# Third attention: scores contract 64 rows in two row halves of the array, 32 keys wide, and the steps go in twos

## The reference, cut to what matters

```python
def _L3_xattn_ref(x, context, Wq, Wk, Wv):      # DIM = 256, NHEADS = 32, HEAD_DIM = 8
    q = x @ Wq.T
    k_raw = context @ Wk.T
    v_raw = context @ Wv.T
    ...
    q = _rmsnorm(q)
    k = _rmsnorm(k)
    scores = jnp.einsum('bhnd,bhmd->bhnm', q, k) * HEAD_DIM ** (-0.5)
    attn = jax.nn.softmax(scores, axis=-1)
    out = jnp.einsum('bhnm,bhmd->bhnd', attn, v)
```

## Time and profile before

| | us |
|---|---|
| median of 3 runs (2715.6 to 2722.59) | 2721.63 |
| the profiled execution | 2722.91 |
| its span, first to last instruction | 2720.8 |
| the 16 pairs of the attention in it, first exponential to end of the last | 526.9 |

### The profile page before, as it was taken

How to read it: one execution, slowest core, us unless ns; L and a number is a source line. 1 busy time by engine, 2 the same in 40 slices (tenths; PEclk the granted TensorE clock), 3 DMA queues, 4 the chain that set the end, 5 groups by cost and what they waited for, 6 DMA issues and landing times. The chain is left out here.

```text
span 2720.8 us, 48003 instructions
## 1 busy us (share of the span) xinstructions
PE 2525.6 (93%) x16164; PEld 1750.9 (64%) x16226; DVE 1721.4 (63%) x3340; ACT 1483.9 (55%) x3294; POOL 1355.3 (50%) x917
## 2 busy tenths in 40 slices
PE   6889999979999999999999999998697799999997
PEld 4567777747777777777777777776454344444443
DVE  4345667657787887787787788786115555554435
ACT  2235444435555566555656655554113667676895
POOL 0025645425666676666667666665102466656300
PEclk9889999999999999999999999998798899999999
DMA  4212222220001000010001000003101000000100
GB/s 155 78 54 85 89 89 76 75 110 16 1 17 45 17 16 17 1 45 17 17 16 44 17 1 17 17 32 154 42 12 58 17 15 17 15 17 15 48 2 16
DMA packets 42437, 108.33 MB, mean 40 GB/s; under 512 B 5044, under 2 KB 26040, under 8 KB 37048
## 3 DMA queue, kind: packets, MB, share of 16 engines
q1 hardware_dynamic: 40424, 102.41, 11.2%
q0 software_dynamic: 768, 2.10, 0.2%
q10 hardware_dynamic: 1008, 0.79, 0.1%
HBM read 99.91 MB, written 4.98 MB: 39 GB/s over the span
## 5 line engine op out<-in xcount | busy, mean ns | idle before, releaser
L1212 POOL TENSOR_TENSOR xn<-xn,l_p 128x512 f32<-128x512 f32 (+1 forms) x400 | 633.9, 1585 | 178.8 <-ACT l_p L1254 162.3
L2213 ACT ACTIVATE l_p<-psum 128x1024 f32<-128x1024 f32 x416 | 394.5, 1022 | 132.6 <-PE psum L2333 132.4
L1340 DVE TENSOR_TENSOR l_plo<-l_p,l_phi 128x512 fp32r<-128x512 f32 (+1 forms) x464 | 405.5, 875 | 63.1 <-ACT l_p L1254 42.4
L1253 ACT ACTIVATE l_phi<-psum 128x512 fp32r<-128x512 f32 (+1 forms) x464 | 279.4, 602 | 221.5 <-PE psum L447 142.1
L1389 DVE TENSOR_REDUCE l_mx<-psum 128x1 f32<-128x512 f32 (+2 forms) x512 | 306.0, 617 | 38.3 <-PE psum L1553 37.8
L2187 POOL TENSOR_TENSOR l_rs<-l_ms,half_power 128x32 f32<-128x32 f32 x45 | 245.1, 5456 | 86.0 <-DVE l_ms L2238 86.0
L1254 ACT ACTIVATE l_p<-psum 128x512 f32<-128x512 f32 (+1 forms) x464 | 281.5, 607 | 0.0
L2333 PE MATMUL psum<-l_qT,l_kT 128*32 128x512 f16 x3328 | 256.4, 384 | 3.3 <-DVE l_qT L2094 2.9
L2343 PE MATMUL psum<-l_p,l_vs 128*32 128x256 f32 x3328 | 254.5, 380 | 0.3 <-ACT l_p L2213 0.3
L1483 PE MATMUL psum<-l_m,l_ones 128*128 128x512 f32 (+1 forms) x464 | 233.3, 503 | 0.0
L1572 PE MATMUL psum<-l_w,l_ctx 128*128 128x256 f32 (+1 forms) x832 | 217.1, 383 | 9.1 <-ACT l_qa L1271 5.4
(11 more groups left out here) (378 smaller groups left out, 5160.0 us busy)
## 6 DMA issues: line engine op xcount, KB each, us to landing
w_stage<-in_L_w_dram SPq DMA_DIRECT2D x76, 384.0 KB, 3.1
l_w<-in_L_w_qkv_dram SPq DMA_DIRECT2D x16, 1024.0 KB, 4.8
l_ct<-in_ctx_tiles_dram SPq DMA_DIRECT2D x52, 128.0 KB
c_T<-in_ctx_T_dram SPq DMA_DIRECT2D x4, 1601.0 KB
l_ctx<-in_ctx_T_dram SPq DMA_DIRECT2D x4, 1601.0 KB, 6.9
c_N<-in_ctx_dram SPq DMA_DIRECT2D x4, 1536.0 KB
s_wg<-in_L_gate_dram SPq DMA_DIRECT2D x4, 1024.0 KB, 12.3
s_wu<-in_L_up_dram SPq DMA_DIRECT2D x4, 1024.0 KB, 14.3
```

Source lines behind the costliest of these rows:

```text
L1212: g_.tensor_tensor(l2_acc[k][0:r, :], first[0:r, :], l2_p[c % 3][0:r, :], ALU.add)\
L1253: act.activation(l2_phi[c % 3][0:r, :], src, ACT.Exp).then_inc(l2_e, 1)
L1340: v.tensor_tensor(l2_plo[c % 3][0:r, :], l2_p[c % 3][0:r, :], l2_phi[c % 3][0:r, :].bitcast(F32), ALU.subtract)\
L2213: act.activation(l3_p[ring[c]][:, :], psum[:, (c % 2) * 2 * BANK:(c % 2 + 1) * 2 * BANK], ACT.Exp, scale=float(D3) ** -0.5).then_inc(l3_e, 1)
```

## The change

Three parts, all in the third attention's inner loop on PE and ACT.

1. `scores` contracts the 64 rows of its two heads only: rows 0 to 63 for heads 0 and 1, rows 64 to 127 for heads 2 and 3. The array is used in eight tiles of 64 rows by 32 columns, and the loops are turned round (`r` outside, `a` inside).
2. `pair` on PE goes in twos: scores of c + 2 and c + 3, values of c and c + 1, then what was due beside c and c + 1.
3. Probabilities `l3_p` go round four buffers without exception (`ring`), and ACT's loop turns over two pairs at a time. The four buffers were there before.

```diff
-        ring = [0, 1, 2, 3] * (C3 % 3) + [0, 1, 2] * ((C3 - 4 * (C3 % 3)) // 3)
+        def ring(i, c):
+            return (i * C3 + c) % 4
...
-            def pair(b, i):
+            def pair(b, i, odd):
                 for c in range(C3):
 
-                    act.wait_ge(l3_s, i * C3 + (b * (NP * C3) + c + 1))
-                    act.activation(l3_p[ring[c]][:, :], psum[:, (c % 2) * 2 * BANK:(c % 2 + 1) * 2 * BANK], ACT.Exp,
+                    act.wait_ge(l3_s, i * (2 * C3) + (b * (NP * C3) + odd * C3 + c + 1))
+                    act.activation(l3_p[ring(odd, c)][:, :], psum[:, (c % 2) * 2 * BANK:(c % 2 + 1) * 2 * BANK], ACT.Exp,
                                    scale=float(D3) ** -0.5).then_inc(l3_e, 1)
...
                 need(pe, l3_e, i * C3 + (b * (NP * C3) + c - 1))
-                for a in range(2):
-                    queries = l3_qT[b % 2][:, n, 2 * a:2 * a + 2, :].rearrange("p h s -> p (h s)")
-                    for r in range(0, P, 32):
+                for r in range(0, P, 32):
+                    for a in range(2):
+                        rows = slice(a * 2 * W3, (a + 1) * 2 * W3)
+                        queries = l3_qT[b % 2][rows, n, 2 * a:2 * a + 2, :].rearrange("p h s -> p (h s)")
                         mm = pe.matmul(bank(c % 2 * 2 + a)[r:r + 32, :],
-                                       l3_kT[b % 2][:, n, j * P + r:j * P + r + 32], queries, start=True, stop=True)
+                                       l3_kT[b % 2][rows, n, j * P + r:j * P + r + 32], queries, start=True, stop=True)
...
                 proj_at, pair_at, turn_at = BESIDE
-                for c in range(C3):
-                    if c + 2 < C3:
-                        scores(b, i, c + 2)
-                    elif not last:
-                        scores(b, i + 1, c + 2 - C3)
-                    values(b, i, c)
-                    if c == OUT_AT:
-                        out(b, i, 0, new, last)
-                    if b == B - 1:
-                        f3_beside(pe, i, c)
...
+                for first in range(0, C3, 2):
+                    for c in (first + 2, first + 3):
+                        if c < C3:
+                            scores(b, i, c)
+                        elif not last:
+                            scores(b, i + 1, c - C3)
+                    for c in (first, first + 1):
+                        values(b, i, c)
+                    for c in (first, first + 1):
+                        if c == OUT_AT:
+                            out(b, i, 0, new, last)
+                        if b == B - 1:
+                            f3_beside(pe, i, c)
```

More of the change, by code:

```diff
@@ L1920, in program @@
         assert PT * (NP - 1) == MC - 1 and N3 - PT * (NP - 1) <= PT
-        ring = [0, 1, 2, 3] * (C3 % 3) + [0, 1, 2] * ((C3 - 4 * (C3 % 3)) // 3)
-        assert len(ring) == C3
+        assert C3 % 2 == 0 and (2 * C3) % 4 == 0 and NP % 2 == 0
+        def ring(i, c):
+            return (i * C3 + c) % 4
         l3_wq = sb("l3_wq", [P, DC, D], F32, l3)
@@ L2207, in l3x_scalar @@
             first_scalar(act)
-            def pair(b, i):
+            def pair(b, i, odd):
                 for c in range(C3):
-                    act.wait_ge(l3_s, i * C3 + (b * (NP * C3) + c + 1))
-                    act.activation(l3_p[ring[c]][:, :], psum[:, (c % 2) * 2 * BANK:(c % 2 + 1) * 2 * BANK], ACT.Exp,
+                    act.wait_ge(l3_s, i * (2 * C3) + (b * (NP * C3) + odd * C3 + c + 1))
+                    act.activation(l3_p[ring(odd, c)][:, :], psum[:, (c % 2) * 2 * BANK:(c % 2 + 1) * 2 * BANK], ACT.Exp,
                                    scale=float(D3) ** -0.5).then_inc(l3_e, 1)
             for b in range(B):
-                with act.Fori(0, NP) as i:
-                    pair(b, i)
+                with act.Fori(0, NP // 2) as i:
+                    for odd in range(2):
+                        pair(b, i, odd)
         def l3x_vector(v):
@@ L2343, in values @@
                     mm = pe.matmul(bank(4 + a, S)[h * 32:(h + 1) * 32, :], l3_vs[a][:, j, h, :],
-                                   l3_p[ring[c]][:, h * S:(h + 1) * S], start=(j == 0), stop=(j == MC - 1))
+                                   l3_p[ring(i, c)][:, h * S:(h + 1) * S], start=(j == 0), stop=(j == MC - 1))
                 mm.then_inc(l3_pv, 1)
@@ L2360, in pair @@
                 proj_at, pair_at, turn_at = BESIDE
-                for c in range(C3):
-                    if c + 2 < C3:
-                        scores(b, i, c + 2)
-                    elif not last:
-                        scores(b, i + 1, c + 2 - C3)
-                    values(b, i, c)
-                    if c == OUT_AT:
-                        out(b, i, 0, new, last)
-                    if b == B - 1:
-                        f3_beside(pe, i, c)
[L2371 to L2377, removed]
+                for first in range(0, C3, 2):
[11 more added lines that the diff above has]
+                            f3_beside(pe, i, c)
+                        for m, context in l3_tiles(last) if new is not None else []:
+                            if c == proj_at[m]:
+                                project(new, i, m, context, last)
+                            if c == turn_at[m]:
+                                turn(b, new, i, m)
+                    if last and new is not None and first + 2 >= C3:
+                        for c in range(2):
+                            scores(new, 0, c)
                 out(b, i, 1, new, last)
```

## The result

The changed kernel takes 2727.97 us (median of 20 runs, 2721.17 to 2730.98), the kernel before 2719.99 us in the same series (20 runs, 2715.6 to 2723.83): ratio 1.0025, 95% interval 1.0019 to 1.0031. So it is 8.0 us by the medians, slower by a quarter of a percent, and inside the 0.3% that the prediction calls no change. The profiled execution took 2728.46 us, its span is 2726.7. Outside the 16 pairs the two traces differ too: 2191.9 us now, 2194.0 before. Over the nine traces of this document that part goes from 2187.0 to 2194.0, while plain pairs of the same code repeat within 0.03 us, so small differences are read from the pairs.

What follows compares the result with a forecast made beforehand. The prediction took a loop of PE and ACT over two PSUM buffers, plus stalls at beside work, as the bound. Pair differences of +1.2 on 2722.9 gave 2724.1, the median 1.3 lower: 2723 us, range 2710 to 2747.

Steps and rivals of the forecast that it cites:

- Row halves overlap, 0.216 us: Scores on PE: the two row halves run side by side, so a step's scores take 0.216 us instead of 0.432.
- halves one after the other: Rival for the scores on PE: row halves do not overlap, scores stay 0.432, +26 us, 2748; chance 0.1.
- A change of tiling costs 0.094: PE between scores and values: each switch between 64 by 32 and 128 by 32 tiles costs 0.094 us.
- The free change: Rival on PE: tiling changes cost 0, the array may not drain, -8.3 us, 2713; chance of faster 0.17.
- the one of 0.2: Rival on PE: a tiling change is dearer, at 0.2 us +13 us in all, 2735; dearer change has chance 0.25.
- The twos: plain loop 3.83 us per four steps: Plain steps of PE and ACT: both values lie in the loop, 0.957 us a step, plain steps lose 0.04 each.
- The sum, +1.2: All 16 attention pairs: full -2.0, last of a batch -0.9, first +1.1, last batch +3.0, together +1.2 us.
- the prediction's list: Full pair's stalls above the floor at beside work, from `out` with project 0 to turn 3: 12.18 before, 11.81 after.
- The clock: Rival for PE in the attention: clock expected at 1.00, a few dips cost little; chance 0.03.
- Signs of being wrong: Profile: values-to-scores gap over 0.35, x8 scores still 0.6 long, exponentials under 0.91 apart, attention clock under 1.00.
- ACT's floor: ACT's exponentials with scores ready: 0.92 us apart; at 0.91 another 1 us faster.
- when PE is behind: Between neighbouring stalls: a group of two takes PE 1.49 us, ACT 1.84, so PE makes up 0.35.

Runs made afterwards that it cites:

- e3: The changed kernel with the loops of the scores the old way round (`a` outside, `r` inside): 2726.25 us, ratio 1.0025.
- e1: The changed kernel with PE's steps one by one, as before the change, scores still of 64 rows: 2711.36 us, ratio 0.9967.
- e2: The changed kernel with scores over all 128 rows again, PE still in twos: 2748.82 us, ratio 1.011.
- e5: The changed kernel, but the first of the 16 pairs has its scores over 128 rows: 2729.77 us, ratio 1.0029.
- e6: The changed kernel with mostly single steps, twos at 0, 2, 8, 10, 16, 18, 20, beside work before values at 0 and 16: 2702.99 us, ratio 0.9927.
- e7: e6 with groups of three at projects (scores, project, two scores, three values), five probability buffers, ACT's loop written out: 2692.15 us, ratio 0.9884.

## Why the prediction was right, point by point

The forecast was no change, 2723 us, and the time is 2727.97, 8.0 us above before, at the edge of what the prediction calls no change. The mechanism, a gain of the halved scores that the loop of the twos pays back, was right. The size was +1.2 us and came out as +7.9 in the attention.

**Row halves overlap, 0.216 us.** Shown: eight start within 0.02 us and are over in 0.41 instead of 0.61, and e3 shows that their order is without effect. The rival "halves one after the other" is out.

**A change of tiling costs 0.094.** Borne out as the prediction reads it, from the last start to the next start (0.33 with rounding and stagger, 0.31 expected). The Trainium skill ("TensorEngine Tiling (Array Packing)", Key Properties) says that changing the tiling mode drains the engine; a price of 0.09 us agrees with a short drain. For a sum the whole step counts, and there two changes cost 0.26 (e1), not 0.19. Of the 0.07 more, 0.02 is that eight scores don't start at one instant (2658.23 to 2658.25), and the values behind them take more as well, next point. The free change and the one of 0.2 are both out.

**The twos: plain loop 3.83 us per four steps.** The mechanism is shown twice: the wait of 0.32 us on the second scores, and e2's +29.7. The size was a little low: the exponentials of the plain stretch start at 2656.14, 2657.06, 2658.22, and the pattern repeats at 3.9. The terms, from the rows above: exponential end to second scores 0.15 (0.145 predicted), to the values 0.34 (0.314), to the next scores 1.00 (0.97), from there to ACT 0.49 (0.46), then 0.92 and 1.02. Each of the three middle terms is 0.03 too small. In the first and third it is the 0.02 over which the eight scores start. The prediction names this term beside its bounds (0.216 plus 0.03) and leaves it out of the sum. In the second it is the 0.02 over which four values start, and the first four of them, which take 0.24 and not 0.216.

**The sum, +1.2.** This is the term that was mis-sized. By kind of pair, predicted and measured difference: six full pairs -2.0, +0.3; three last pairs -0.9, -0.7; the first pairs of the later batches +0.6, +1.3; the last batch +3.0, +4.3; the very first pair +0.5, +2.7. The first four kinds miss by 4.5 us together, the last is the clock. ACT in a full pair, the second, shows where the 4.5 come from:

```profile
2172.68 1.94 ACT L2216 ACTIVATE l_p<-psum 128x1024 f32<-128x1024 f32 x2 [0.69 <-PE psum L2338]
2175.22 1.94 ACT L2216 ACTIVATE l_p<-psum 128x1024 f32<-128x1024 f32 x2 [0.60 <-PE psum L2338]
2178.69 3.77 ACT L2216 ACTIVATE l_p<-psum 128x1024 f32<-128x1024 f32 x4 [1.53 <-PE psum L2338]
2184.51 3.77 ACT L2216 ACTIVATE l_p<-psum 128x1024 f32<-128x1024 f32 x4 [2.05 <-PE psum L2338]
2190.74 3.77 ACT L2216 ACTIVATE l_p<-psum 128x1024 f32<-128x1024 f32 x4 [2.46 <-PE psum L2338]
2196.97 3.77 ACT L2216 ACTIVATE l_p<-psum 128x1024 f32<-128x1024 f32 x4 [2.46 <-PE psum L2338]
2201.24 1.94 ACT L2216 ACTIVATE l_p<-psum 128x1024 f32<-128x1024 f32 x2 [0.50 <-PE psum L2338]
2204.32 3.77 ACT L2216 ACTIVATE l_p<-psum 128x1024 f32<-128x1024 f32 x4 [1.15 <-PE psum L2338]
```

The time from one row's start to the next, less 0.92 for each exponential, is the stall above the floor. The first two rows make one entry of the prediction's list; in its order the stalls measured 2.33, 2.14, 2.55, 2.55, 0.59, 1.24 and 0.78, 12.18 in all instead of 11.81. All but one are 0.03 to 0.09 above the prediction, as steps and loop that are each a few hundredths too short would make them. That is 0.38 us a full pair (36.11 against 35.73).

Two entries of the sum were also uneven in themselves. Three times 33.54 to 33.3 is -0.7 and not -0.9. And the last batch has +0.75 a pair, while the prediction's own 0.04 a step gives 1.04, 4.2 for the four, against 4.3 measured. That this comes so near is luck: the loop measured 0.06 a step longer than before, but not every step of these pairs is a plain one.

**The clock.** The prediction expected a few dips to cost little. The first pair at half clock was 2.6 us longer than its like in the second batch (38.53 and 35.93), 0.6 before (35.86 and 35.26), so 2.0 us of the difference are the clock's, and the table in e5 bears this out.

**Signs of being wrong.** Two of the four that the prediction names did come. The clock was 0.90 in the first pair. And behind a stall exponentials start 0.90 apart (2179.61 and 2180.51), so ACT's floor is a little under the prediction's 0.92; at most 0.2 us a pair, in the kernel's favour. Neither touches the mechanism.

**Where the expected gain of the 64 rows went.** It is paid back in the loop. Halved scores give 22 us in twos; the twos themselves cost 29.7. The gain "when PE is behind" was there: the stall at `out` with project 0 fell from 2.97 to 2.33. But project 1, turn 1 with project 3, `out` at step 16 and turn 3 each lost about 0.17, and the full pair is even.

## What to carry to other kernels

When two engines pass work to and fro over two buffers, count what stands in the loop behind each wait before making an instruction cheaper. The twos put 0.86 us of values behind a wait to save a change of tiling. With 64 rows they cost 16 us against single steps that change twice as often (534.8 and 518.8), and 30 us where there was no change to save. Price a change from rows where PE waits for nothing, and over a whole step: the gap alone showed 0.09, the step 0.13. In e6 and e7 two moves went with the further gain: long foreign pieces right behind the instructions that feed the other engine, and work that nobody waits for after the next feed, there with one more buffer.

## What the runs showed of the hardware

- Eight tiles of 64 rows by 32 columns, fp16, 512 columns, run as one: 0.41 us for all, in either order of issue.
- A change between 64 by 32 and 128 by 32 tiling cost as much as one between 128 by 32 and 128 by 128 (0.33 by rounded starts against 0.31); with PE waiting for nothing, two per step made 0.65 us of streams into a step of 0.91.
- Half clock lasted 7.7 us into the attention in the changed kernel and 2.8 us in the one before, with PE busy 6.56 of 7.66 and 2.48 of 2.84 us there. Over nine traces, 2.8 to 8.2 us of half clock made the first pair 0.4 to 2.9 us longer. What sets the moment of its end stayed open.
- Exponentials of 128 by 1024 elements whose scores were ready started 0.90 to 0.92 us apart, while one takes 1.02: each starts before the one ahead of it has ended.
